# Output projection of the first two tiles sliced into the last two attention steps, and the second attention written out tile by tile

## The reference, cut to what matters

```
x  = layernorm(x + softmax(q k^T / sqrt(32)) v @ ow + ob)         q,k,v = x @ qkvw + qkvb
x  = layernorm(x + fake_quant(x) @ fake_quant(ctx[batch]))        fake_quant: clip(round(x/s + z), 0, 255), then (q - z) * s
x  = layernorm(x + x @ W_base^T + b_base + experts(x))            8 experts of rank 16, the best 2 by router, softmax weights
```

## Time and profile before

| | us |
|---|---|
| median of 3 runs (lowest, highest) | 775.95 (775.20, 775.99) |
| the profiled execution's own time | 774.92 |
| its span, first to last instruction | 773.1 |
| PE busy | 730.0 (94%) |
| DVE busy | 480.1 (62%) |
| ACT busy | 428.6 (55%) |
| POOL busy | 201.3 (26%) |
| mean granted clock of TensorE | 0.974 |

### The profile page before, as it was taken

How to read it: one execution, slowest core, us unless ns; L and a number is a source line. 1 busy time by engine, 2 the same in 40 slices (tenths; PEclk the granted TensorE clock), 3 DMA queues, 4 the chain that set the end, 5 groups by cost and what they waited for, 6 DMA issues and landing times.

```text
span 773.1 us, 11949 instructions
## 1 busy us (share of the span) xinstructions
PE 730.0 (94%) x3567; PEld 536.0 (69%) x3576; DVE 480.1 (62%) x852; ACT 428.6 (55%) x925; POOL 201.3 (26%) x149
## 2 busy tenths in 40 slices
PE   6989999999999999999999996989999977999996
PEld 5767766766866867866866842467667655888884
DVE  6876755755745745745755742555766778566554
ACT  5457667667766866866866884543334471212111
POOL 6260320420420420420420000033433374122111
PEclk9999999999999999999999986899999998999999
DMA  8665444444454353353333754363454121112101
GB/s 295 200 166 173 117 131 142 113 136 139 109 165 112 107 177 101 109 180 98 108 111 87 218 185 148 98 241 124 155 186 139 55 84 55 67 70 101 62 28 55
DMA packets 55553, 99.45 MB, mean 129 GB/s; under 512 B 11104, under 2 KB 22112, under 8 KB 54624
## 3 DMA queue, kind: packets, MB, share of 16 engines
q1 hardware_dynamic: 55232, 98.65, 41.6%
q10 hardware_dynamic: 288, 0.39, 0.2%
HBM read 56.54 MB, written 16.91 MB: 95 GB/s over the span
## 4 chain that ended last, share of the span: by engine, by line
PE 61%; issue 16%; DVE 8%; POOL 5%; DMA 4%; SPq 3%; ACT 2%; POOLq 0%; DVEq 0%; ACTq 0%
PE bank L457 36%; PE bank L518 8%; PE bank L544 8%; PE bank L558 6%; POOL xb L1093 2%; DVE st L1310 2%; POOL mv L1043 1%; SPq L233 1%; DMA ctx_scratch<-ctxs 1%; DMA xres<-in_x 1%; PE bank L476 1%; DVE x1s L1408 1%; PE bank L672 1%; DMA w_raw<-in_wqkv 1%; POOL xres L1038 1%
## 5 line engine op out<-in xcount | busy, mean ns | idle before, releaser
L800 ACT ACTIVATE probs<-bank 128x512 f32<-128x512 f32 x256 | 154.5, 605 | 127.6 <-PE bank L544 124.9
L1230 DVE TENSOR_REDUCE m_col<-bank 128x1 f32<-128x512 f32 x256 | 172.9, 688 | 76.9 <-PE bank L518 76.3
L805 ACT ACTIVATE bank<-bank,m_col 128x512 f32<-128x512 f32 x256 | 171.3, 669 | 13.8 <-DVE m_col L1230 12.9
L457 PE MATMUL bank<-big_hi,w_hi 128*128 128x512 f32 x384 | 156.7, 408 | 6.3 <-DVE big_lo L1123 6.0
L457 PE MATMUL bank<-big_lo,w_hi 128*128 128x512 f32 x384 | 152.3, 397 | 0.0
L457 PE MATMUL bank<-big_hi,w_lo 128*128 128x512 f32 x384 | 150.9, 393 | 0.0
L544 PE MATMUL bank<-qp,kp 98*128 98x512 f32 x256 | 108.3, 424 | 2.7 <-DMA qp<-m_row 2.4
L518 PE MATMUL bank<-kp,qp 96*128 96x512 f32 x256 | 105.8, 413 | 1.9 <-ACT bank L805 1.9
L457 PEld LDWEIGHTS bank<-big_hi,w_hi 128*128 128x128 f32 x384 | 73.2, 191 | 25.2 <-DVE big_lo L1123 6.0
L1027 POOL TENSOR_SCALAR c_raw<-c_raw,sc 128x1024 f32<-128x1024 f32 x16 | 19.2, 1200 | 255.0 <-DMA c_raw<-in_ctx 250.3
L457 PEld LDWEIGHTS bank<-big_hi,w_lo 128*128 128x128 f32 x384 | 72.8, 189 | 17.0
(11 more groups left out here) (137 smaller groups left out, 1003.9 us busy)
## 6 DMA issues: line engine op xcount, KB each, us to landing
...
qp<-q_hi SPq DMA_DIRECT2D x128, 64.0 KB, 2.0
...
```

What stands on the lines that cost most here:

```text
L457: mm = nc.tensor.matmul(dst, lhs[a], rhs[b], start=(k == 0 and n == 0) if first is None else False, stop=(k == last_k and n == 2))
L800: nc.scalar.activation(probs[:, j, t, :], bank(ST0 + i % 2), ACT.Exp).then_inc(sem["exp_ok"], 1)
L805: nc.scalar.activation(bank(MAX[n % 3]), bank(MAX[n % 3]), ACT.Exp, bias=m_col[:, n:n + 1], accum_out=l_col[:, 1 - par, n:n + 1]).then_inc ...
L1230: nc.vector.reduce_max(m_col[:, n:n + 1], bank(MAX[n % 3]), AX, negate=True).then_inc(sem["rowmax"], 1)
```

## The change

- **Tiles 0 and 1 in steps 16 and 17.** `out_group(n, h, k)` is one slice (three matmuls) of half tile h of tile n. Step 16 puts the 14 slices k = 0 to 6 of the first halves of tiles 0 and 1 behind its scores, from the seventh pair on; step 17 puts the 14 of the second halves and the four slices k = 7 behind its transposed scores. The last eighth of a tile's input (k = 7) comes straight from `ctxs` on chip (DVE, `split_last_group`), so the context of unit 14 is no longer stored to DRAM.
- **POOL splits.** The weight `ow` (16 pieces, two instructions each) and tiles 0 to 3 are split by POOL instead of ACT and DVE. Four homes for `cx_hi`, `cx_lo`.
- **SP's order.** In step 15 the load of the quantised context (2 MB) is gone from between the pack DMAs; behind them come tiles 0 and 1, a store, the second half of `ow`, the reciprocals of unit 14, the 2 MB, tiles 2 and 3, and then the maxima of step 16 (`store_shift`). Residual rows are loaded only after the last context product, since `xres` now lies where `probs` was.
- **Second attention unrolled.** Tiles go in token order (four of one batch, then four of the other), with an order per engine that is written out. Banks are given by `out_banks`. The column sums move here (before tile 3 and before tile 6), `context_product` runs one tile later, and its row-sum matmuls are gone: ACT's `centre_c1` sums while it writes c1. `quantise` is one DVE instruction (before: two); the clip at 0 is ACT's Relu. DVE's `invert_sums` of unit 15 stands ahead of `divide` of unit 14.
- **Last stage's first tile inside it.** `transpose_x2(0)` and `hidden(0)` stand around the context product of tile 6. The second half of W_base is loaded only after the last output projection, straight over the low part of `ow`.

```diff
+        homes = [(192, 196), (80, 84), (108, 112), (116, 120)]
+        cx_hi = [at(f"cx_hi{q}", a, [P, KT, P], f32r) for q, (a, _) in enumerate(homes)]
+        cx_lo = [at(f"cx_lo{q}", b, [P, KT, P], f32r) for q, (_, b) in enumerate(homes)]
...
+        out_banks = ((1, 2), (0, 7), (3, 4), (1, 2), (0, 7), (1, 2), (0, 7), (1, 2))
...
+            load_tile(0)
+            load_tile(1)
             store_context(UNITS - 3, 1, G - 2)
...
+            load_ow(1, 3 * UNITS)
+            store_recip(UNITS - 2)
+            spread_recip(UNITS - 2)
+            load_c2(0)
+            load_tile(2)
+            load_tile(3)
+            store_shift(UNITS, 0)
             store_recip(UNITS - 1)
             spread_recip(UNITS - 1)
...
+            sp.wait_ge(sem["pv_mm"], UNITS)
+            load_residual(0)
+            load_residual(1)
             store_context(UNITS - 1, 1, G - 1)
...
+            load_residual(2)
+            load_residual(3)
+            sp.wait_ge(sem["ctx_out"], 16 * (UNITS - 1))
+            load_tile(4)
+            sp.wait_ge(sem["a_mm"], 2)
+            load_c2(1)
...
+            def out_group(n, h, k):
+                if k == 0 and h == 0:
+                    if n < NT // 2:
+                        pe.wait_ge(sem["cx_lo_ok"], n + 1)
+                    else:
+                        pe.wait_ge(sem["cx_split"], n + 1 - NT // 2)
+                    if n == 1:
+                        pe.wait_ge(sem["v_ok"], UNITS)
+                    elif n == 2:
+                        pe.wait_ge(sem["ctx_ok"], UNITS - 1)
+                    elif n == 3:
+                        pe.wait_ge(sem["r1_ok"], 1)
+                    elif n >= 4:
+                        pe.wait_ge(sem["r1_ok"], n - 2 if n == 4 else n - 1)
+                    if n == 6:
+                        pe.wait_ge(sem["corr_ok"], NB)
+                if k == 0 and h == 1:
+                    if n < 2:
+                        pe.wait_ge(sem["sum_ok"], NS * UNITS)
+                    elif n == 2:
+                        pe.wait_ge(sem["exp_ok"], NS * UNITS)
+                if n == 0:
+                    pe.wait_ge(sem["ow_lo"], h * KT + k + 1)
+                if k == KT - 1 and n < NT // 2:
+                    pe.wait_ge(sem["cx7_lo"], n + 1)
+                home = n if n < 2 else 2 + n % 2
+                mm = split_mm(bank(out_banks[n][h]), (cx_hi[home][:, k, :], cx_lo[home][:, k, :]),
+                              (big_hi[:, k, h * 512:(h + 1) * 512], big_lo[:, k, h * 512:(h + 1) * 512]), k, KT - 1)
+                if k == KT - 1:
+                    mm.then_inc(sem["a_mm" if h else "a_half"], 1)
...
+                def scores_and_first_tiles():
+                    groups = [(n, 0, k) for n in range(2) for k in range(KT - 1)]
+                    done = 0
                     for n in range(NS):
-                        if maxima:
-                            score(n)
+                        score(n)
                         if n == 2:
...
                         score_t(n)
...
-                                sums += 1
-                    if maxima:
-                        maxima_to_rows()
+                        until = 0 if n < 6 else 2 * (n - 5) if n < 9 else n - 1 if n < NS - 1 else len(groups)
+                        while done < until:
+                            out_group(*groups[done])
+                            done += 1
+                    maxima_to_rows()
+                    context()
+                def last_scores_and_first_tiles():
+                    groups = [(n, 1, k) for n in range(2) for k in range(KT - 1)] + [(n, h, KT - 1) for n in range(2) for h in range(2)]
+                    for done in range(2):
+                        out_group(*groups[done])
+                    recip_to_rows()
+                    done = 2
+                    for n in range(NS):
+                        score_t(n)
+                        while done < min(n + 3, len(groups)):
+                            out_group(*groups[done])
+                            done += 1
                     context()
                 early = isinstance(s, int) and 1 <= s <= 2
                 if maxima and not early:
...
             def transpose_c1(m):
                 pe.wait_ge(sem["c1_ok"], m + 1)
-                if not isinstance(m, int) or m >= 1:
+                if m == 0:
+                    pe.wait_ge(sem["r1_half"], 3)
+                else:
                     pe.wait_ge(sem["c1T_ok"], m)
...
+            for h in range(2):
+                out_project(2, h)
+            column_sums(0)
+            transpose_c1(0)
+            for h in range(2):
+                out_project(3, h)
+            transpose_c1(1)
+            context_product(0)
+            transpose_c1(2)
+            out_project(4, 0)
+            context_product(1)
+            out_project(4, 1)
+            transpose_c1(3)
+            context_product(2)
+            for h in range(2):
+                out_project(5, h)
+            column_sums(1)
+            transpose_c1(4)
+            context_product(3)
+            for n in (6, 7):
+                for h in range(2):
+                    out_project(n, h)
+                transpose_c1(n - 1)
+                context_product(n - 2)
             transpose_x2(0, 0, 0)
+            context_product(6)
+            hidden(0)
...
+            def centre_c1(n):
+                act.wait_ge(sem["qp2"], n + 1)
+                if n == 0:
+                    act.wait_ge(sem["ctx_out"], 16 * (UNITS - 1))
+                else:
+                    act.wait_ge(sem["tr_mm"], n)
+                if n >= 2:
+                    act.wait_ge(sem["k1"], n - 1)
+                nc.scalar.activation(c1[:, :], quant[:, :], ACT.Identity, bias=consts[:, 3:4], accum_out=c1_sum[:, n % 2:n % 2 + 1]).then_inc(sem["c1_ok"], 1)
...
+            def split_ow(h, k):
+                cols = slice(h * S, (h + 1) * S)
+                pool.wait_ge(big_in[h][k], 48 - 16 * h)
+                nc.gpsimd.tensor_scalar(big_hi[:, k, cols], big_raw[:, k, cols], 1.0, 0.0, ALU.mult, ALU.add).then_inc(sem["ow_hi"], 1)
+                pool.wait_ge(sem["ow_hi"], h * KT + k + 1)
+                nc.gpsimd.tensor_tensor(big_lo[:, k, cols], big_raw[:, k, cols], big_hi[:, k, cols].bitcast(f32), ALU.subtract).then_inc(sem["ow_lo"], 1)
+            def split_tile(n):
+                home, q, ks = n if n < 2 else 2 + n % 2, n % 2, slice(0, KT - 1)
+                pool.wait_ge(by_parity["a_in"][q], 16 * (n // 2 + 1))
+                if n == 0:
+                    pool.wait_ge(sem["ctxq_ok"], UNITS)
+                elif n == 1:
+                    pool.wait_ge(sem["proj_done"], 3 * UNITS)
+                elif n == 2:
+                    pool.wait_ge(sem["pv_mm"], UNITS - 1)
+                else:
+                    pool.wait_ge(sem["st_mm"], NS * UNITS)
+                nc.gpsimd.tensor_scalar(cx_hi[home][:, ks], cx_raw[:, q, ks], 1.0, 0.0, ALU.mult, ALU.add).then_inc(sem["cx_pool"], 1)
+                pool.wait_ge(sem["cx_pool"], n + 1)
+                nc.gpsimd.tensor_tensor(cx_lo[home][:, ks], cx_raw[:, q, ks], cx_hi[home][:, ks].bitcast(f32), ALU.subtract).then_inc(sem["cx_lo_ok"], 1)
...
+            def residual_sum(n):
+                dve.wait_ge(sem["xr_ok"], n + 1)
+                if n >= 4:
+                    dve.wait_ge(sem["x2_ok"], n - 3)
+                for h in range(2):
+                    cols = slice(h * 512, (h + 1) * 512)
+                    dve.wait_ge(sem["a_mm" if h else "a_half"], n + 1)
+                    nc.vector.tensor_tensor(x1s[n % 4][:, cols], bank(out_banks[n][h]), xres[:, n % 2, cols], ALU.add).then_inc(sem["r1_ok" if h else "r1_half"], 1)
+                dve.wait_ge(sem["r1_ok"], n + 1)
+                dve.wait_ge(sem["r1_half"], n + 1)
+                stats(x1s[n % 4], 0, n + 1, "st1", "mv1", "ve1")
+            def quantise(n):
+                dve.wait_ge(sem["qp1"], n + 1)
+                nc.vector.tensor_scalar(quant[:, :], quant[:, :], QMAX, MAGIC, ALU.min, ALU.add).then_inc(sem["qp2"], 1)
...
+                minus_mean(1 + m % 2, m + 1, "rstd2", "nm2")
+            residual_sum(0)
+            first_mean(0)
+            quantise(0)
+            residual_sum(1)
+            first_mean(1)
+            row_correction(0)
+            column_correction(0)
+            quantise(1)
+            residual_sum(2)
```

865 lines of the change are left out of this document (435 added, 430 removed).

## The result

| | kernel before | changed kernel |
|---|---|---|
| median of the runs | 775.58 us (773.9 to 775.99, 4 runs) | 758.54 us (757.49 to 759.26, 4 runs) |
| ratio, 95% interval | | 0.9777 (0.9762 to 0.9791) |
| profiled execution, its span | 774.92, 773.1 us | 757.49, 755.7 us |

It is 17.0 us faster. Forecast were 753.8 us and 22 less, with 745 to 765 as the range. Direction, mechanism and range held; the gain is 5 us smaller than forecast.

A forecast was written before the change was run, and what follows sets the result against it. TensorE was taken to bound the kernel, with idle or half-speed stretches to fill. Terms 501.9 + 120.1 + 8.7 + 1.75 + 7 = 639.5 against 661.6, 22.1 us less, gave 753.8 us; range 745 to 765.

The forecast's parts named there:

- What bounds: Whole kernel: TensorE bounds it, but has idle or half-speed time near 450 to 500 and 625 to 652 us.
- Nothing is gained: Rival, steps 16 and 17: TensorE really was busy, so 96 added matmuls cost the 22 us saved later; 775 us, chance 0.03.
- the clock stays at half: Rival, steps 16 and 17: the added slices don't raise TensorE's clock, 26 us more; 780 us, chance 0.05.
- Steps 16 and 17: Slices go in after a 4.1 us wait for tile 0; step 17 ends at 501.9 instead of 499.8, costing 2.1 us.
- First chain: At the first transpose_c1: TensorE waits 8.7 us for residual rows and passes behind them, then 1.75 us for half clock.
- TensorE's work behind step 17: From step 17's end to the last stage's second tile: matmuls, transposes and context products counted at 120.1 us together.
- The change to the last stage: Remaining TensorE waits there taken as 7 us, against 9.7 of waits and 3.75 of clock before; bounds 1 and 14.
- the three waits: At the last stage's start: split of x2T about 2 us, W_base's last pieces 3 late, routing and hwT 1.
- Tiles 3 to 7: Second attention: 15.6 us of TensorE work a tile, each c1 ready 4 to 8 us before its transpose; cost 0.
- the rival on the port: DVE and POOL block each other on the path, 2 us on five tiles and 3 at the change; 767, chance 0.17.
- The 44 us of splits on GpSimd: Splits moved to POOL, called no free gift because DVE and POOL can exclude each other for a whole instruction.

The follow-up runs named there:

- experiment 1: Changed kernel with the 32 slices of output tiles 0 and 1 taken out of steps 16 and 17 and put behind step 17; 772.06 us, ratio 0.9938.
- experiments 3: Changed kernel with the transpose of c1(0) moved into the middle of the second half of output tile 3; 753.06 us, ratio 0.9692.
- 7: Changed kernel with 31 unread matmuls on constants put into TensorE's wait in front of the first transpose of c1; 756.97 us, ratio 0.977.
- 8: Changed kernel with residual rows of tiles 0 and 1 loaded in step 17 into their own buffer, output bias added earlier; 753.03 us, ratio 0.9706.
- 9: Changed kernel with transpose_c1(0) inside output tile 3's second half and tile 4's first half in front of transpose_c1(2); 750.54 us, ratio 0.9668.
- experiment 4: Changed kernel with the row-sum matmuls put back in front of each context product of the last stage, unread; 758.37 us, ratio 0.9764.
- experiment 6: Changed kernel with GpSimd's addition of the correction row to the residual sum done on one column only; 756.09 us, ratio 0.9752.

## Why the prediction was right, and where it was short

**What bounds.** Right. The stretch read as room (22 matmuls in 13 us at 0.52) was room: with the slices out, experiment 1 gives back 13 of the 17 us, in the DMA order of the changed kernel. "Nothing is gained" is refuted by the 17 us, and "the clock stays at half" by 0.99 and 1.00 in the two steps.

**Steps 16 and 17.** The wait 3.92 against 4.1, the landing 3.9 against 4.5; from step 15's product (446.5 before, 447.6 after) to the end of step 17, 55.8 against the forecast's 55.4. Mechanism and size right. 1.1 us of the miss was there already at step 15. It arises before 76 us, where thirteen traces spread over 1.9 us, all of them later than the one of before; whether the changed program starts later or the one trace was early stays open.

**First chain.** Right in place and cause: 7.54 against 8.7, half clock 1.6 against 1.75 (experiments 3, 7, 8 and 9).

**TensorE's work behind step 17.** Here a term was mis-sized. A context product was read off a row of 15 matmuls as 3.24 us; it takes 3.45. Ten such groups were counted, 2.1 us. Read off the same row, the removal of the row sums looks like 0.4 us a tile; experiment 4 measures 0.20.

**The change to the last stage.** 7 was forecast; 6.7 us of waits and 2.6 of half clock are 9.3. The forecast named the three waits, but gave the clock nothing of its own behind them, and the routing is held by the port (experiment 6).

**Tiles 3 to 7.** Right, no wait over 1 us; so the rival on the port is refuted as a matter of every tile. VectorE's passes did stand still there (2.77 us at 544.11 and 3.43 at 584.23 for an addition that takes 1.23 alone), but the cover held. The 44 us of splits on GpSimd that the forecast names are 40 by the earlier trace rows (16 x 1.74 and 4 x 3.04); no term of the sum uses them.

The differences: +1.1 at the start, +0.4, -1.2 and -0.2, +2.1, +2.3 make 4.5 of the 5.1 us between 639.5 and 644.6; 0.6 is spread over small shifts.
